# A two-layer attention kernel on one core: the second product of four units issued in one piece at the end of each step

## The chip, the cores and the metric

The kernel runs on one core of a Trainium2 chip. The metric is device time in microseconds (us) for one execution of the whole program; lower is better. The kernel before has a median of 1084.87 us over three runs (1084.28 to 1086.7).

## What is computed

Two transformer layers over one sequence of 2048 tokens with 128 channels, in float32, with an adaptive layer norm (scale and shift from a condition vector) ahead of every block.

- Layer 0 attention: 16 heads of width 8, over all 2048 keys, no mask. For each head `softmax(q k^T / sqrt(8)) v`, then an output product.
- Layer 0 feed-forward: a router picks one of 16 experts for each token; the chosen expert (`up * silu(gate)`, then down) and a shared expert of width 512 are added.
- Layer 1 attention: 8 query heads of width 16 with one shared key and value head, causal.
- Layer 1 feed-forward: a token-shifted channel mix with a squared ReLU and a sigmoid gate.

Only the attention of layer 0 is touched by the change. Its core is, for 512 queries and four heads at a time:

```python
w = jnp.einsum('bshd,bzhd->bhsz', q, k) / jnp.sqrt(jnp.float32(DV))
w = jax.nn.softmax(w, axis=-1)
vw = jnp.einsum('bhsz,bzhd->bshd', w, v)      # the second product
```

## The kernel before

**Units and steps.** Layer 0's attention is cut into 16 units (numbers 0 to 15). A unit is 512 queries and four heads. A unit has 16 steps, one for each block of 128 keys. The steps of layer 0 are numbered 0 to 255 in the program's order, so units 12 to 15 are steps 192 to 255. Layer 1 follows with eight units.

**What a step does for each unit.** A step J forms the scores of its 128 keys against 512 queries, turned so that keys lie on the partitions. That is done in two pairs of heads, called `st` 0 and `st` 1 here (`emit_st`, L425; the matmuls are at L919). Each pair is two bf16 matmuls of 512 columns. They work in different rows of the array, and each fills one bank of PSUM. ScalarE (ACT) takes the exponential of each bank (L1464), one instruction a bank, four a step, into an SBUF tile `PT`, and so frees the bank.

The second product (`pv`, L931 to L948) multiplies the exponentials with the values and adds into the bank `O`. It is float32, one product for each of the four heads, placed in four column strips of the array. The profile counts two MATMUL instructions for each float32 product. The second product of step J is issued in step J+1 (`LAG = 1`).

**The row maxima.** The exponentials need the maximum of every row. For this the same scores are formed once more, untransposed, for a later unit: a "score tile" S (L878 for layer 0, L885 and L888 for layer 1). It is 128 queries by 512 keys for two heads, in a double bank S0 or S1. VectorE (DVE) reduces it (L1218) and so frees the bank. In steady state a step holds two S tiles for the unit after this one. Near the end of layer 0 there are none for seven steps (236 to 242), since layer 1's keys are not there yet. From step 243 the S tiles are layer 1's first ones, which are small.

**Banks.** The transposed scores and all small pieces of other work take the banks T0, T1 and T2 in turn (`next_t`, L84). A bank may be written again only when its reader has freed it. A pair `st` takes two of the three. So where nothing else takes a bank in between, one of the two banks of `st` 1 is the first bank of `st` 0 of the same step.

**The order of the work** is written out by a planner, `make_plan`. Every engine walks the one list `order` and does its own part of each entry, strictly in that order. Loop L499 writes the order for the steps. In layer 0, where a score tile is due (`k` over 0, from `rate`, L459), a step is:

`light work; [piece]; st 0; S; pv of J-1, queries 0-255; light work; [piece]; st 1; S; pv of J-1, queries 256-511`

Here a `[piece]` is at most one piece of other work that is due (`do_later`, L445). I call the slot ahead of `st` 1 the middle slot. The slot ahead of `st` 0 is the end slot of the step before, since it stands behind that step's last second product. Where no score tile is due (steps 236 to 242), and in layer 1, the second product is already issued in one piece at the end of the step (L530): `st 0; (S); [piece]; st 1; (S); pv of J-1, all 512 queries`.

**Pieces of other work in units 12 to 15:** turning and projecting the attention's output (L957, L967, L976), the layer norm's transpose (L834), the router's logits (L1009), sorting the tokens by expert (L1037 to L1042), the shared expert (`up`: L1017 and L1018, `down`: L1027), and the sorted experts: `m0` (a transpose, L1049, in a T bank, copied by ACT at L1548), `m1` (L1061, in an S bank) and `m2` (L1069, in a T bank, copied by ACT at L1558). Later come layer 1's projections (L847, L864). SyncE fetches the experts' weights and stores and loads sorted rows. GpSimd (POOL) scatters and gathers them.

Of the kernel before, what the change touches and what calls it, by code (L numbers as in the profile page):

```python
# [18 lines left out]
LAG = 1  # L19
# [23 lines left out]
def kts(L, u):  # L43
    return 16 if L == 0 else 4 * (UNITS[1][u][0] + 1)
# [66 lines left out]
def make_plan():  # L111
# [44 lines left out]
    def between(key, *a):  # L156

        b = next_s()
        P.take((key,) + a, b, (b + "a", b + "b"))
        if key in ("up", "m1"):  # L160
            P.gate[(key,) + a] = len(P.gate) + 1
        P.stage(key, *a)
# [190 lines left out]
    def may_score():  # L353
        if si[0] >= len(tiles):
            return False
        return may_begin(*tiles[si[0]][:2])

    def emit_s():
        if not may_score():
            return  # L360
        t = tiles[si[0]]
        si[0] += 1
        L, u = t[:2]
        between("s", *t)
        if si[0] == len(tiles) or tiles[si[0]][:2] != (L, u):
            P.stage("neg", L, u)

            def neg_turn():
                P.take(("neg", L, u), P.next_t())
                P.stage("neg_turn", L, u)  # L370
                out[L, u] = 1
            urgent.append((now[0] + 2, neg_turn))
# [16 lines left out]
    def finish(L, u):  # L389
        c, quad = UNITS[L][u]  # L390
        last = quad == QUADS[L] - 1
        if (L, u) == units[-1]:
            tail()
            return
        P.stage("os", L, u)

        def o_turn():
            (between if L == 1 and u < 6 else beside)("o_turn", L, u)
            if last:
                at(now[0] + (2 if u < 15 else 1), w_turn)  # L400

        def w_turn():
            beside("w_turn", L, c)
            at(now[0] + 1, y)

        def y():
            P.take(("y", L, c), P.next_t())
            P.stage("y", L, c, P.xb)
            after_chunk(L, c, now[0])
        at(now[0] + 2, o_turn)  # L410

    def emit_pv(J, halves):
        if not 0 <= J < len(steps):
            return
        L, u, kt = steps[J]
        if kt == 0 and halves[0] == 0:
            P.take(("o", L, u), "O", filled=False)
        P.stage("pv", L, J - STEPS0 * L, u, kt, halves)
        if halves[-1] == 1:
            P.pvs += 1  # L420
            if kt == kts(L, u) - 1:
                P.pv[L, u] = P.pvs
                finish(L, u)

    def emit_st(J, pair):  # L425
        if J >= len(steps):
            return
        L, u, kt = steps[J]
        j = J - STEPS0 * L
        if L == 1 and kt >= 4 * UNITS[1][u][0]:  # L430
            P.masks[L, j, pair] = len(P.masks) + 1
        if (L, u) == (1, 7):
            P.wide.add((L, j, pair))
            P.take(("st", L, j, 2 * pair), next_s())
        else:
            for i in range(2):
                P.take(("st", L, j, 2 * pair + i), P.next_t())
        P.stage("st", L, j, u, kt, pair)

    def do_light(half=0):  # L440
        for k in sorted(k for k in light if k <= now[0] + half):
            for fn in light.pop(k):
                fn()

    def do_later():  # L445

        if urgent and urgent[0][0] <= now[0]:
            urgent.pop(0)[1]()
            return
        for book in (later, after):  # L450
            k = min(book, default=now[0] + 1)
            if k <= now[0]:
                fn = book[k].pop(0)
                if not book[k]:
                    book.pop(k)
                fn()
                return

    def rate(L, J):  # L459

        k = 0
        for J2 in range(J, min(J + 24, len(steps))):
            due = sum(n for n, s0, of in zip(many, starts, units) if s0 - LEAD[of] <= J2 and may_begin(*of))
            k = max(k, -(-(due - si[0]) // (J2 - J + 1)))
        return min(k, MOST[L]) if may_score() else 0
# [33 lines left out]
    while J < len(steps) + LAG:  # L499
        L, u, _ = steps[min(J, len(steps) - 1)]  # L500
        do_light()
        if J == begun[L, u] and not out[L, u]:
            for _ in range(4):
                emit_s()
            do_later()
            now[0] += 1
            continue
        k = rate(L, J)
        do_later()
        emit_st(J, 0)  # L510
        if L == 0 and k:
            emit_s()
            emit_pv(J - LAG, (0,))
            do_light(0.5)
            do_later()
            emit_st(J, 1)
            for _ in range(k - 1):
                emit_s()
            emit_pv(J - LAG, (1,))
        else:  # L520
            if k:
                emit_s()
            do_light(0.5)
            do_later()
            emit_st(J, 1)
            if k > 1:
                emit_s()
            if (L, u) >= (0, 15):
                do_later()
            emit_pv(J - LAG, (0, 1))  # L530
            for _ in range(k - 2):
                emit_s()
        now[0] += 1
        J += 1
# [27 lines left out]
def adaln_two_layers(nc, A, out):  # L562
    ctx = ExitStack()
    P = make_plan()
    order, turn = P.order, P.turn
    with ctx:
# [1393 lines left out]
```

## Time and profile before

| | |
|---|---|
| median of the runs | 1084.87 us |
| the profiled execution | 1091.35 us |
| its span, first to last instruction | 1089.5 us |
| PE (TensorE matmul) busy | 1007.8 us, 93% |
| DVE busy | 896.7 us, 82% |
| ACT busy | 823.0 us, 76% |
| chain that ended last | PE 70%, DVE 11%, ACT 8% |
| the second product's matmuls in that chain (L948) | 26% |

The profiled execution is 6.5 us (0.6%) over the median of the runs and 1.85 us over its own span. Busy time is time in which an engine had an instruction in flight. Matmuls overlap one another at their ends, so the distance between two starts is the cost in a dense stretch, not the duration. In a row of the timeline the first number is the start in us from the beginning of the span, the second the time from the group's start to its end. What stands in square brackets is how long the engine had been idle, and what it waited for.

### The profile page before, as it was taken

The page shows a single profiled execution, that of the slowest core. Times are in us where ns is not written, and L with a number is a line of the kernel's source. Part 1 is how long each engine was busy: PE and PEld are TensorE (multiplying, and loading weights), DVE is VectorE, ACT ScalarE, POOL GpSimd, SP SyncE. Part 2 cuts the span into 40 slices and gives each one's busy share as a digit, 9 for nine tenths or more (in the row PEclk, how much of TensorE's full clock was granted, in tenths as well). Part 3 has the DMA queues.
Part 4 walks back from the last instruction along what each step waited for, and adds up shares of the span by engine and source line. Part 5 has one row for each costly group of instructions (what it writes and reads, how often), then busy time and mean ns, then how long its engine had stood idle before and what let it go on. Part 6 is the DMA issues. An engine that isn't in the chain of part 4 may idle for free.

```text
span 1089.5 us, 22136 instructions
## 1 busy us (share of the span) xinstructions
PE 1007.8 (93%) x8642; PEld 340.8 (31%) x8642; DVE 896.7 (82%) x1135; ACT 823.0 (76%) x1585; POOL 195.2 (18%) x370
## 2 busy tenths in 40 slices
PE   3979999999999999999998899989989998899997
PEld 2332222222222222222222244334343563323313
DVE  5899999999999999999988677775778767897503
ACT  3229999998999998999986587666755576656785
POOL 4533200003000003000023200231042113110102
PEclk9569999999999999999999899999999999999996
DMA  3470620100000000000001522105200431200000
GB/s 109 115 167 4 134 43 12 21 2 2 2 3 2 2 1 2 3 1 2 3 1 39 176 79 59 40 27 97 37 1 7 142 106 37 34 10 1 1 11 10
DMA packets 47693, 42.05 MB, mean 39 GB/s; under 512 B 6534, under 2 KB 45798, under 8 KB 47590
## 3 DMA queue, kind: packets, MB, share of 16 engines
q1 hardware_dynamic: 45190, 35.17, 13.1%
q0 software_dynamic: 1824, 5.25, 1.7%
q8 instruction: 69, 1.13, 0.4%
q14 instruction: 34, 0.28, 0.1%
q10 hardware_dynamic: 576, 0.23, 0.1%
HBM read 26.83 MB, written 13.30 MB: 37 GB/s over the span
## 4 chain that ended last, share of the span: by engine, by line
PE 70%; DVE 11%; ACT 8%; issue 4%; SPq 3%; DMA 2%; POOL 1%; another core or an unknown queue 1%; POOLq 0%; ACTq 0%; DVEq 0%
PE O L948 26%; PE T L919 14%; PE S L878 8%; DVE mx L1218 6%; ACT PT L1464 5%; PE S L885 4%; PE T L928 4%; PE S L1061 2%; SPq L1840 2%; PE S L1027 1%; ACT PT L1458 1%; PE S L1017 1%; PE T L1069 1%; PE S L928 1%; PE T L957 1%
## 5 line engine op out<-in xcount | busy, mean ns | idle before, releaser
L1218 DVE TENSOR_REDUCE mx<-S 128x2 f32<-128x1024 f32 (+2 forms) x672 | 759.6, 1180 | 79.5 <-PE S L878 31.5
L1464 ACT ACTIVATE PT<-T 128x512 f32<-128x512 f32 (+2 forms) x1280 | 675.8, 580 | 117.9 <-PE T L928 49.1
L948 PE MATMUL O<-PT,Va 128*9 128x256 f32 (+1 forms) x4032 | 317.7, 387 | 3.3 <-ACT Os L1499 3.3
L878 PE MATMUL S<-Ks,Qs 48*128 48x512 bf16 x1024 | 206.3, 396 | 17.4 <-DVE mx L1218 8.4
L919 PE MATMUL T<-Qs,Ks 51*128 51x512 bf16 x1024 | 202.1, 387 | 13.4 <-ACT PT L1464 8.1
L919 PEld LDWEIGHTS T<-Qs,Ks 51*128 51x128 bf16 x1024 | 56.1, 93 | 224.8 <-issue 128.8
L948 PEld LDWEIGHTS O<-PT,Va 128*9 128x9 f32 x4032 | 59.8, 88 | 207.1 <-issue 197.5
L885 PE MATMUL S<-K,Qs 96*128 96x512 bf16 (+3 forms) x320 | 89.4, 349 | 5.0 <-DVE mx L1218 3.9
L928 PE MATMUL T<-Qs,K 99*128 99x512 bf16 (+3 forms) x256 | 67.4, 344 | 12.0 <-ACT PT L1464 8.3
L948 PE MATMUL O<-PT,V 128*17 128x512 f32 (+3 forms) x640 | 74.9, 534 | 0.0
L878 PEld LDWEIGHTS S<-Ks,Qs 48*128 48x128 bf16 x1024 | 52.6, 95 | 41.1 <-DVE mx L1218 27.3
L1725 POOL CAST n<-nm 128x16 bf16<-128x16 f32 x24 | 5.5, 228 | 316.6 <-DVE nm L1226 316.4
L1631 POOL TENSOR_SCALAR_AFFINE_SELECT PT<-PT 128x256 f32<-128x256 f32 x64 | 25.8, 409 | 132.6 <-ACT PT L1464 103.8
L885 PEld LDWEIGHTS S<-K,Qs 96*128 96x128 bf16 x320 | 28.3, 97 | 48.2 <-DVE mx L1218 18.9
L1740 POOL TENSOR_TENSOR vw<-om,rl 128x128 f32<-128x128 f32 x16 | 6.5, 407 | 185.6 <-DVE rl L1232 185.6
L928 PEld LDWEIGHTS T<-Qs,K 99*128 99x128 bf16 x256 | 19.3, 98 | 49.7 <-issue 36.8
L1458 ACT ACTIVATE PT<-S 128x1024 f32<-128x1024 f32 (+3 forms) x32 | 28.4, 943 | 3.2 <-PE S L928 3.0
L888 PE MATMUL S<-mq,idb 128*128 128x128 bf16 x128 | 25.7, 220 | 0.0
L1181 DVE RECIPROCAL rl<-T 128x4 f32<-128x4 f32 x3 | 0.5, 170 | 28.7 <-PE T L984 28.7
L1785 POOL DMA_INDIRECT XP<-sorted_y,posu x16 | 15.8, 990 | 38.7 <-DMA sorted_y<-Vf 34.5
L1449 ACT ACTIVATE nrow<-T 12x512 bf16<-12x512 bf16 x24 | 14.1, 586 | 11.4 <-PE T L898 11.1
L1277 DVE SCALAR_TENSOR_TENSOR Vf<-Vf,S 128x512 f32<-128x512 f32 x16 | 10.9, 682 | 13.8 <-ACT Vf L1542 12.8
(283 smaller groups left out, 814.1 us busy)
## 6 DMA issues: line engine op xcount, KB each, us to landing
Qs<-in_L_ffn_experts SPq DMA_DIRECT2D x28, 192.0 KB, 2.7
Ks<-in_L_ffn_experts SPq DMA_DIRECT2D x20, 192.0 KB, 2.6
Vf<-sorted_x SPq DMA_DIRECT2D x12, 256.0 KB, 4.3
sorted_y<-Vf SPq DMA_DIRECT2D x12, 256.0 KB, 2.3
Qs<-rows_q SPq DMA_DIRECT2D x24, 128.0 KB, 4.5
rows_q<-q SPq DMA_DIRECT2D x7, 384.0 KB, 2.5
Qs<-rows_q SPq DMA_DIRECT2D x36, 64.0 KB
sorted_x<-XP POOLq DMA_DIRECT2D x1, 1792.0 KB, 10.7
```

Of the source, the lines that this page charges most:

```text
L878: m = e.matmul(two[:, i, :], Qs[r0:r0 + 48, hp, q0:q0 + 128], Ks[r0:r0 + 48, hp, CH * kb:CH * kb + CH], start=True, stop=True, tile_positi ...
L885: m = e.matmul(two[:, i, 0:n], Q1[0:96, 4 * quad + 2 * pair + i, q0:q0 + 128], K1[0:96, CH * kb:CH * kb + n], start=True, stop=True)
L888: m = e.matmul(two[:, i, n - 128:n], idb[:, :], mq[:, :], start=False, stop=True, skip_group_check=True)
L919: m = e.matmul(bank, Ks[r0:r0 + 51, hp, keys], Qs[r0:r0 + 51, hp, CH * c:CH * c + CH], start=True, stop=True, tile_position=(r0, 0))
L928: m = e.matmul(bank[:, lo:CH], K1[0:99, keys], Q1[0:99, 4 * quad + 2 * pair + i, CH * c + lo:CH * c + CH], start=True, stop=True)
L948: m = e.matmul(Ob[32 * g:32 * g + d1, lo:hi], v, PT[(2 * j + g // 2) % 4][:, p0 + lo:p0 + hi], start=(kt == 0 and halves[0] == 0), stop=Tr ...
L1061: m = e.matmul(two[:, h, 128 * k:128 * k + 128], w_of(g, 2 * p + k)[:, 128 * h:128 * h + 128], hS[p % 2][:, 128 * k:128 * k + 128], start= ...
L1218: e.tensor_reduce(mx[:, u % 2, h0:h0 + 2, kb], two[:, :, 0:n], AX.X, ALU.max).then_inc(free, 1)
L1458: e.activation(both, Sb[turn["st", L, j, 2 * pair][0]][:, :, lo:CH], ACT.Exp).then_inc(free, 1)
L1464: e.activation(PT[(2 * j + pair) % 4][:, CH * i + lo:CH * i + CH], bank[:, lo:CH], ACT.Exp).then_inc(free, 1)
L1631: e.affine_select(out=both, in_=both, compare_op=ALU.is_ge, fill=0.0, base=0, pattern=[[0, 2], [1, 128]], channel_multiplier=-1).then_inc( ...
L1840: e.dma_start(Ks[r0:r0 + 8 * many, heads, cols], src[:, heads, :]).then_inc(loaded, 16)
```

## The change

In steps of units 12 to 15 in which a score tile is due, the second product is no longer issued as two pieces (queries 0-255 between the first S tile and the middle slot, queries 256-511 at the end of the step). It is issued as one piece of 512 queries at the end of the step. Everything else keeps its place in the order, and the banks are taken in the same turn. Units 0 to 11 keep the two pieces.

```diff
         do_later()
         emit_st(J, 0)
         if L == 0 and k:
+
+            halves = ((0,), (1,)) if u < 12 else ((), (0, 1))
             emit_s()
-            emit_pv(J - LAG, (0,))
+            if halves[0]:
+                emit_pv(J - LAG, halves[0])
             do_light(0.5)
             do_later()
             emit_st(J, 1)
             for _ in range(k - 1):
                 emit_s()
-            emit_pv(J - LAG, (1,))
+            emit_pv(J - LAG, halves[1])
```

## Rows read from the trace of the kernel before

**Rows 1.** Busy time by window (us, each engine's busy us and instructions, PEclk): unit 11, unit 12.
```profile
504.50:542.10 37.60, 37.04 (x394) 8.58 (x392) 37.10 (x35) 35.87 (x68) 1.27 (x5) 1.00 0.01 2
542.10:590.80 48.70, 45.34 (x450) 14.22 (x446) 44.65 (x63) 39.54 (x76) 12.23 (x18) 1.00 0.01 3
```

**Rows 2.** The page's costliest group: operation, shapes, count, busy us, mean ns, idle before.
```profile
L1218 DVE TENSOR_REDUCE mx<-S 128x2 f32<-128x1024 f32 (+2 forms) x672 | 759.6, 1180 | 79.5 <-PE S L878 31.5
```

**Rows 3.** Timeline (start, us, engine, line): a step without pieces, TensorE, up to the next.
```profile
556.13 0.39 PE L919 MATMUL T<-Qs,Ks 51*128 51x512 bf16 x2
556.35 0.40 PE L878 MATMUL S<-Ks,Qs 48*128 48x512 bf16 x2
556.67 0.62 PE L948 MATMUL O<-PT,Va 128*9 128x256 f32 x8
557.23 0.39 PE L919 MATMUL T<-Qs,Ks 51*128 51x512 bf16 x2
...
558.39 0.39 PE L919 MATMUL T<-Qs,Ks 51*128 51x512 bf16 x2
```

**Rows 4.** Timeline, TensorE: step 238, in which the second product is already one piece.
```profile
721.23 0.39 PE L919 MATMUL T<-Qs,Ks 51*128 51x512 bf16 x2
722.39 0.39 PE L919 MATMUL T<-Qs,Ks 51*128 51x512 bf16 x2 [0.78 <-ACT PT L1464]
722.71 1.05 PE L948 MATMUL O<-PT,Va 128*9 128x512 f32 x8
723.69 0.66 PE L834 MATMUL T<-idf,XP 128*128 128x128 f32 x4
```

**Rows 5.** Timeline: a step with m0 and m2 in the middle slot, m1 at its end.
```profile
646.58 0.39 PE L919 MATMUL T<-Qs,Ks 51*128 51x512 bf16 x2
...
647.00 1.08 ACT L1464 ACTIVATE PT<-T 128x512 f32<-128x512 f32 x2 [0.38 <-PE T L919]
...
648.14 0.38 ACT L1548 ACTIVATE Vf<-T 128x256 f32<-128x256 f32 x1
...
648.67 0.39 PE L919 MATMUL T<-Qs,Ks 51*128 51x512 bf16 x2
...
649.76 1.16 PE L1061 MATMUL S<-Vf,Qs 128*128 128x128 f32 x8
...
650.85 0.39 PE L919 MATMUL T<-Qs,Ks 51*128 51x512 bf16 x2
```

**Rows 6.** Timeline, TensorE: start of step 192, first piece, last piece and end of step 203.
```profile
539.68 0.39 PE L919 MATMUL T<-Qs,Ks 51*128 51x512 bf16 x2
...
544.46 0.66 PE L957 MATMUL T<-idf,Os 128*128 128x128 f32 x4
...
572.20 1.12 PE L1017 MATMUL S<-hT,sgT 128*128 128x512 f32 x2
...
574.12 0.39 PE L919 MATMUL T<-Qs,Ks 51*128 51x512 bf16 x2
```

**Rows 7.** Timeline, TensorE: start of step 209, and a wait in step 212.
```profile
590.73 0.39 PE L919 MATMUL T<-Qs,Ks 51*128 51x512 bf16 x2
...
605.40 0.39 PE L919 MATMUL T<-Qs,Ks 51*128 51x512 bf16 x2 [1.00 <-issue]
```

**Rows 8.** Busy time by window, columns as in rows 1: the stretch at the lower clock.
```profile
612.00:618.00 6.00, 5.43 (x36) 0.75 (x34) 4.87 (x5) 3.44 (x7) 0.00 (x0) 0.50 1.07 300
```

**Rows 9.** Timeline, TensorE: starts of a step with m1 in the middle, and the next.
```profile
634.20 0.39 PE L919 MATMUL T<-Qs,Ks 51*128 51x512 bf16 x2
...
638.47 0.39 PE L919 MATMUL T<-Qs,Ks 51*128 51x512 bf16 x2
```

**Rows 10.** Timeline, TensorE: starts of the two pairs of a step of unit 15.
```profile
771.24 0.39 PE L919 MATMUL T<-Qs,Ks 51*128 51x512 bf16 x2
...
772.66 0.39 PE L919 MATMUL T<-Qs,Ks 51*128 51x512 bf16 x2
...
774.19 0.39 PE L919 MATMUL T<-Qs,Ks 51*128 51x512 bf16 x2
```

## The prediction

> **What bounds the kernel now.** I read the page's busy shares and chain of waits first: PE is 93% busy and holds most of the chain that ended last. Shares say nothing of one stage, so I then took busy time by window, one unit each. In unit 11, which has no other work, DVE is busy 37.10 of 37.60 us, PE 37.04 and ACT 35.87 [rows 1]: three engines are nearly full, and a step of 2.35 us is two reductions of 1.18 us [rows 2]. From unit 12 on there is other work. The unit takes 48.7 us, DVE has 4 us free, PE 3.4 us, ACT 9 us [rows 1]. From step 216 to the end of layer 0 the timeline shows TensorE nearly dense, so what lengthens its queue lengthens the kernel.
>
> Next I read one step as distances between starts. In a plain step `st` 0 costs 0.22 us, the S tile 0.32, a half of the second product 0.56, and then `st` 1 begins, 1.10 us after `st` 0; the next step begins 2.26 us after the first [rows 3]. TensorE's own part of this is 2 x (0.22 + 0.31 + 0.55) = 2.16 us.
>
> **Which steps change.** Units 12 to 15 are 64 steps. Steps 236 to 242 have no score tile due and already issue one piece. So 57 steps change.
>
> **What one merged piece costs.** In step 238 the merged product starts at 722.71, and the next instruction at 723.69: 0.98 us [rows 4]. Two halves are 2 x 0.55 = 1.10 us [rows 3]. TensorE's own work falls by 0.12 us a step, or 57 x 0.12 = 6.8 us in all. That is the whole gain. The Trainium skill (TensorE: Matmul & The Clock Gate, "Back-to-back issue gap") puts the fixed part of an isolated matmul at about 2.5 ns, by which merging would save only some 0.02 us a step for its eight instructions fewer; the rows show six times that, and by the page's figure the sum below would be 5.7 us higher.
>
> **What the half in the middle was covering.** `st` 1 needs two of three T banks, and with an empty middle slot one of them is the first bank of `st` 0. ACT starts the exponential 0.42 us after `st` 0 (647.00 against 646.58), two take 1.08 us together and overlap a little, so one runs about 0.6 us [rows 5]; then TensorE has to hear of it. In step 238, which has an empty middle slot, this sum is seen directly: `st` 1 starts 1.16 us after `st` 0, and TensorE was idle 0.78 us waiting for the exponential [rows 4]. So the shortest first half is 1.16 us whatever TensorE does. Now the S tile and the half product fill 1.08 of these 1.16 us. After the change only `st` 0 and S (0.53 us) lie there, and the other 0.63 us is idle, unless a piece stands in the middle slot. The second half of the step becomes 0.22 + 0.31 + 0.98 = 1.51 us, against 1.08: +0.43 us, whatever follows.
>
> So a step changes by 0.43 us plus (new first half - old first half). A step without a middle piece goes from 2.16 us of TensorE's time to 1.16 + 1.51 = 2.67 us, or +0.51 us, less the waits for DVE that it has today and that the slower pace hides.
>
> **No cover from elsewhere.** Nothing else is moved: no DMA, no ACT, DVE or POOL instruction changes its place, and SP's queue is untouched. On PE's queue the half is moved past the middle slot, `st` 1 and one S tile. Those three start earlier where their banks allow. The completion that ACT waits for (the whole product of the step before) is still at the end of the step.
>
> **The sum, by stretches.**
>
> *Steps 192 to 203* (12 steps, empty middle slots). From 539.68 to 574.12 they take 34.44 us [rows 6]. Behind them stand six pieces (0.59, 0.59, 1.09, 0.56, 1.00 and `up` with 1.92 us, from start to next start; the first and the last in [rows 6]): 5.75 us. After: 12 x 2.67 + 5.75 = 37.8 us. In three steps ACT first copies a piece and `st` 1 comes 0.17 to 0.35 us later than 1.16; these stay, 0.7 us. 38.5 - 34.4 = **+4.0 us**. The waits of today (34.44 - 12 x 2.16 - 5.75 = 2.8 us) are what DVE held back; at 2.67 us a step DVE needs 2.36 us and is no longer the limit.
>
> *Steps 204 to 208* (sorting and two `up` pieces). Waits for DVE of 0.3 to 0.8 us stand behind every `up`. Two of these five steps should gain about nothing (the rank sum in a middle slot takes the half's place, and a DVE wait swallows the rest), the others +0.1 to +0.4: **+0.9 us**, bounds 0 and 5 x 0.43 = 2.2.
>
> *Steps 209 to 215* (590.73 on [rows 7]). Here no engine is busy: PE waits 1.0 us for "issue" at 605.40 [rows 7] while ACT and DVE idle too and the DMA queues carry the expert weights, and then TensorE runs at half clock in 612 to 618 [rows 8]. What ends last is not TensorE's queue, so most of 7 x 0.43 = 3.0 us is absorbed; below nothing is possible too, if the half-clock stretch goes. I take **+1.0 us**, bounds -2 and +3.
>
> *Steps 216 and 217*: empty middle, dense PE, 0.48 and 0.43: **+0.9 us**.
>
> *Steps 218 to 220 and 228 to 232* (8 steps, `m1` in the middle). 4.27 us today [rows 9]. `m1` costs 1.09 us [rows 5], so the first half is 0.53 + 1.09 = 1.62 us, over 1.16: covered. The second S tile wants the bank of the first, whose reduction ends about 0.64 + 1.22 = 1.86 us in, and is then started at about 1.97 instead of 1.84. Total 1.97 + 0.31 + 0.98 + 1.00 = 4.26: **0**, bounds -1 (8 x 0.12) and +1.
>
> *Steps 221 to 226* (6 steps, `m0` and `m2` in the middle). 4.27 us today, `st` 1 at 2.09 without a wait [rows 5]. After: both exponentials run until 1.50, then ACT copies `m0` in 0.38 us [rows 5], and `st` 1 wants `m0`'s bank: 1.88 + 0.14 = 2.02. The first half stays almost as long although TensorE has less to do. Then 0.53 + 0.98 + 1.09 (`m1`) = 2.60 against 2.18 [rows 5]: 4.62, +0.35 each, **+2.1 us**; step 227 has a turn in the middle and both banks of `st` 0 wanted again: **+0.45**.
>
> *Steps 233 to 235*: +0.42 for the first; the other two wait for DVE between `up` pieces anyway, +0.1: **+0.5 us**.
>
> *Steps 243 to 255* (unit 15, layer 1's small S tiles). No wait in most of them. The first half is 1.36 us in the mean of twelve (1.42 in the one shown, 771.24 to 772.66 [rows 10]), since the S tile is longer for TensorE; it can fall to 1.16. 12 x 0.20 = 2.4 us are gained there, and 13 x 0.43 = 5.6 us lost: **+3.2 us**.
>
> Sum: 4.0 + 0.9 + 1.0 + 0.9 + 0 + 2.1 + 0.45 + 0.5 + 3.2 = **+13.0 us**. Against its own time the profiled execution would go from 1091.35 to about 1104.4, its span from 1089.5 to 1102.5. That execution is 6.5 us over the median, and the changed stretch does not hold that difference in a visible place, so I add 13.0 to the median: **1097.9 us**. With every stretch at its lower bound the sum is about +6, at its upper about +19.
>
> **Rivals.**
>
> *TensorE's own arithmetic decides (faster).* If ACT gave the bank back within the 0.53 us that remain, each step would simply lose 0.12 us: -6.8 us, 1078 us. For it: PE's chain share and its dense stretches. Against it: in step 238 the wait is there, 0.78 us [rows 4]. It decides only where a middle piece of over 0.63 us stands that needs no copy ahead of `st` 1, and that is 8 steps of 57. Chance 0.05.
>
> *The slack of units 12 and 13 swallows the loss.* DVE and the DMA stall set the pace to step 215, so that only the dense stretches pay (0.9 + 2.1 + 0.45 + 0.5 + 3.2 = 7.2 us): 1092 us. If the dense stretches too run at their lower bounds, with the 8 steps' gain of 1 us and some gain from the half-clock stretch, about +2, 1087 us. For it: DVE was busy 44.65 of 48.7 us in unit 12 [rows 1]. Against it: 2.67 us is more than DVE's 2.36. Chance 0.15, one in five of it within 0.2%.
>
> *The clock falls.* TensorE would be idle 0.6 us in every plain step. It had been idle often ahead of 612, and then ran at a granted clock of 0.50, 1.2 GHz, in 612 to 618 [rows 8]; at half the clock TensorE's 2.16 us of a plain step could double. Between nothing and 2.2 us more a step I take 1.5, since part falls into waits. If half of the first 24 steps ran so, 12 x 1.5 = 18 us would be added to 13: 1116 us. Against it: step 238 idles 0.78 us ahead of `st` 1, and its `st` still takes 0.39 us as in the plain step at full clock [rows 3, 4]. The Trainium skill (TensorE: Matmul & The Clock Gate, "A second HAM failure mode: psum-queue depth-cycling") says that short idle times between groups of matmuls which cycle through PSUM banks can make the clock swing between its two levels; by it this rival would be the likely one, and step 238, where just this pattern keeps the full clock, speaks against it. Chance 0.06.
>
> *The change does nothing.* If the planner had issued whole products already in these steps, the time would stay. The rows show 256-column products in 57 of the 64. Chance under 0.01; with small absorbed effects of other kinds I leave 0.03 to "no difference".
>
> *One sign more:* the half-clock stretch vanishes (-3 us) together with the slack's absorbing. That lands at 1085 to 1090 and shares the 0.15 above.
>
> **How the numbers follow.** Forecast as summed 0.71; slack swallows 0.15; clock falls 0.06; faster 0.05; nothing 0.03. A run of this kernel can tell about 0.2% (2.2 us) from no change. Faster by more: 0.06 (0.05 and a little of the absorbed case). Within 0.2%: 0.03 + 0.03 = 0.06. Slower by more: 0.88. The range runs from 1089.5 (half-way between the slack case's 1092 and 1087) to 1104.5 (all upper bounds); the faster case and the fallen clock lie outside it.
>
> **What the profile after should show.** (1) L948 in units 12 to 15 as 128x512 groups of about 1.05 us, about 57 more. (2) In plain steps of unit 12, `st` 1 at 1.16 us after `st` 0 with an idle time of some 0.6 us <-ACT PT L1464, and a step of 2.67 us. (3) Steps with `m0` and `m2` in the middle at about 4.6 us, with `m1` in the middle still near 4.27. (4) Steps of unit 15 near 3.1 to 3.2 on the same work instead of 2.95 for the one shown. (5) Layer 1 unchanged, only later. The prediction is wrong if `st` 1 starts well below 1.16 us after `st` 0, if the second half of a step is below 1.5 us, or if TensorE's clock falls in unit 12.

## The result and the profile after

The changed kernel takes 1098.97 us in the median (1097.14 to 1102.02), against 1085.36 us (1084.28 to 1086.7) for the kernel before on the same chip, four runs each. The ratio is 1.0138, interval 1.0122 to 1.0155: 13.6 us slower, where 13.0 were forecast. The profiled execution took 1100.52 us, its span is 1098.7 us.

First the counts. The groups of the second product in layer 0, shapes kept apart (operation, shapes, count, then busy us and mean ns, idle before), show that the change did what it says. The first two lines are after, the third before. Eight instructions are one whole product, so there are 65 of them (520) instead of 8 (64): 57 more.

```profile
L951 PE MATMUL O<-PT,Va 128*9 128x256 f32 x3056 | 237.9, 383 | 3.0 <-ACT Os L1502 3.0
L951 PE MATMUL O<-PT,Va 128*9 128x512 f32 x520 | 68.0, 595 | 0.0
```

```profile
L948 PE MATMUL O<-PT,Va 128*9 128x512 f32 x64 | 8.4, 595 | 0.0
```

The plain step that answers to [rows 3] is the same step 198, on the timeline of TensorE (start, us, engine, line, idle before):

```profile
559.54 0.39 PE L922 MATMUL T<-Qs,Ks 51*128 51x512 bf16 x2
559.76 0.38 PE L881 MATMUL S<-Ks,Qs 48*128 48x512 bf16 x2
560.70 0.39 PE L922 MATMUL T<-Qs,Ks 51*128 51x512 bf16 x2 [0.56 <-ACT PT L1467]
560.91 0.40 PE L881 MATMUL S<-Ks,Qs 48*128 48x512 bf16 x2
561.24 1.05 PE L951 MATMUL O<-PT,Va 128*9 128x512 f32 x8
562.22 0.39 PE L922 MATMUL T<-Qs,Ks 51*128 51x512 bf16 x2
```

The first half of the step, from `st` 0 to `st` 1, is 1.16 us (1.10 in [rows 3]) although TensorE has only 0.53 us of work in it; it stands idle 0.56 us until the exponential is done. The second half, up to the next `st` 0, is 1.52 us (1.16 in [rows 3]). The step is 2.68 us, against 2.26.

What TensorE's matmuls waited for in 540 to 640 us (total us, times, longest), after and then before:

```profile
PE T L922 <- ACT PT L1467: 14.7, 25, 0.9
```

```profile
PE T L919 <- ACT PT L1464: 2.2, 5, 1.1
```

The wait for ACT to give back a T bank has gone from 2.2 to 14.7 us in this stretch. (A second trace of the kernel before, introduced below, has 1.0 us there; the longest of the five waits stood in a disturbed step.) ACT itself is not fuller: in the window of [rows 1] that it calls unit 12, which is steps 193 to 208, it is busy 39.59 us, before 39.54, but these 16 steps take 52.9 us instead of 48.7, at full clock.

```profile
543.40:596.30 52.90, 43.15 (x322) 12.00 (x322) 45.29 (x63) 39.59 (x75) 12.60 (x18) 1.00 0.01 3
```

A step with `m0` and `m2` in the middle slot, which answers to [rows 5]: the second pair starts 1.93 us after the first, the step takes 4.53 us.

```profile
651.25 0.39 PE L922 MATMUL T<-Qs,Ks 51*128 51x512 bf16 x2
651.78 0.44 PE L1052 MATMUL T<-idf,Vf 128*128 128x128 f32 x2
652.34 0.69 PE L1072 MATMUL T<-Qs,Vf 128*128 128x128 f32 x4
...
653.18 0.39 PE L922 MATMUL T<-Qs,Ks 51*128 51x512 bf16 x2
653.72 1.05 PE L951 MATMUL O<-PT,Va 128*9 128x512 f32 x8
654.69 1.16 PE L1064 MATMUL S<-Vf,Qs 128*128 128x128 f32 x8
655.78 0.39 PE L922 MATMUL T<-Qs,Ks 51*128 51x512 bf16 x2
```

### The profile page after: what moved, and what is told of

It reads as the page before. It is cut to its first block, busy times and chain, and to the rows that moved or that the text cites. A ratio compares the mean times of both kernels' runs of the same rounds, so it can differ in the third digit from the quotient of the medians.

```text
span 1098.7 us, 21253 instructions
## 1 busy us (share of the span) xinstructions
PE 1003.0 (91%) x8186; PEld 335.8 (31%) x8186; DVE 896.8 (82%) x1135; ACT 821.9 (75%) x1585; POOL 195.5 (18%) x370
## 4 chain that ended last, share of the span: by engine, by line
PE 69%; DVE 11%; ACT 9%; issue 4%; SPq 3%; DMA 2%; POOL 1%; POOLq 0%; ACTq 0%; DVEq 0%
PE O L951 26%; PE T L922 14%; PE S L881 8%; DVE mx L1221 6%; ACT PT L1467 6%; PE S L888 4%; PE T L931 4%; PE S L1064 2%; PE S L1030 2%; SPq L1843 1%; ACT PT L1461 1%; PE S L1020 1%; DMA Ks<-rows_k 1%; PE S L931 1%; PE T L1072 1%
## 5 line engine op out<-in xcount | busy, mean ns | idle before, releaser
L951 PE MATMUL O<-PT,Va 128*9 128x256 f32 (+1 forms) x3576 | 305.9, 414 | 3.0 <-ACT Os L1502 3.0
L951 PEld LDWEIGHTS O<-PT,Va 128*9 128x9 f32 x3576 | 53.0, 88 | 185.2 <-issue 176.7
L1412 ACT ACTIVATE hT<-T,mc 128x512 f32<-128x512 f32 x15 | 11.6, 775 | 13.1 <-PE T L837 12.8
```

Source lines behind the costliest of these rows:

```text
L951: m = e.matmul(Ob[32 * g:32 * g + d1, lo:hi], v, PT[(2 * j + g // 2) % 4][:, p0 + lo:p0 + hi], start=(kt == 0 and halves[0] == 0), stop=Tr ...
```

## The experiments

Step lengths below are distances between the starts of `st` 0. The expectations use the stretches of the prediction. All times of a table are from one trace each.

### The kernel before, a second trace

The two first traces differ by only 9.2 us in span (5.4 us in steps 192 to 255), the medians by 13.6. Most of the missing part sits in one place: steps 209 to 215 took 33.66 us before and 27.80 us after. So the kernel before was traced again, unchanged.

> The kernel before once more, for a second trace. In its first trace steps 209 to 215 took 33.66 us against 27.80 after the change, with stalls of all engines at 604 and 608 us and a half clock from 612 to 619 us; that trace is also 6 us above the median of the plain runs. Theory (these 6 us are an accident of that one execution): the second trace shows steps 209 to 215 in 24 to 29 us, a profiled time of 1085 to 1088 us, and a difference to the changed kernel of about 13 us step by step. Rival (the stretch is always so slow before the change, and the change gains 6 us there which it loses elsewhere): again about 33 us.

Its profiled time is 1085.81 us, and steps 209 to 215 take 25.95 us. Busy time by window, 604 to 612 us, in the first trace and in this one:

```profile
604.00:612.00 8.00, 5.04 (x38) 1.31 (x30) 3.67 (x4) 3.67 (x7) 3.94 (x5) 1.00 0.42 134
```

```profile
604.00:612.00 8.00, 8.00 (x74) 2.28 (x66) 7.07 (x9) 6.45 (x13) 2.87 (x3) 1.00 0.60 189
```

In the first, PE, DVE and ACT are all held up (busy 5.04, 3.67 and 3.67 of 8 us) while expert weights are being fetched, and the half clock of [rows 8] follows. They are held up in turn rather than together: over steps 209 to 215 there is only 0.33 us in which none of the three is busy. In the second trace there is neither the hold-up nor the half clock. [Rows 7, 8] showed a disturbance that one execution has and another has not.

### The changed kernel, a second trace

> The changed kernel once more, for a second trace. Theory: every step of units 12 to 15 has the length of the first trace to 0.05 us, except where all engines stall together or the granted clock is 0.50; such places (737 to 741 and 918 to 922 us in the first) lie elsewhere or are gone. Rival (the half clock is the change's doing): it comes again at the same place, near 737 us.

Its profiled time is 1107.76 us. It ran on another chip than the first traces, one on which the kernel before takes 1093.17 us. Steps 192 to 208, 216 to 232 and 243 to 255 have the lengths of the first trace to 0.02 us a stretch. Now steps 209 to 215 take 34.95 us, with a half clock from 612 to 622, and step 235 takes 9.51 us instead of 8.61:

```profile
612.00:622.00 10.00, 8.58 (x24) 1.72 (x24) 6.04 (x7) 4.19 (x9) 0.00 (x0) 0.50 0.72 207
```

So the disturbance meets both kernels. The half clock at 737 us came again at 745, in the same step (241, not touched by the change), and cost the same 1.6 us. That much speaks for the rival. But a kernel below whose layer 0 is that of the kernel before has it in step 241 as well, and in the second trace of the kernel before it lies two steps later. So it is not the change's doing. The other three traces from this chip also have 30.4 to 32.7 us in steps 209 to 215, while none of the seven traces on the two chips where the kernel before takes 1083.9 and 1084.5 us has more than 26.1. Step 235 goes with it: it takes 9.1 to 9.8 us in the five traces with slow steps 209 to 215 (the first of the kernel before among them), and 8.5 to 8.6 us in the eight others. The disturbance is in all four traces of the one chip, in none of the seven of the two others, and in one of the two first traces; why is open.

With the two traces that have it in neither place side by side, the second before and the first after, the loss can be read stretch by stretch (us):

| steps | before | after | difference | forecast |
|---|---|---|---|---|
| 192 to 203 | 34.44 | 38.83 | +4.39 | +4.0 |
| 204 to 208 | 16.64 | 16.78 | +0.14 | +0.9 |
| 209 to 215 | 25.95 | 27.80 | +1.85 | +1.0 |
| 216, 217 | 5.53 | 6.10 | +0.57 | +0.9 |
| 218 to 220 and 228 to 232 | 33.01 | 32.33 | -0.68 | 0 |
| 221 to 226 | 25.63 | 27.34 | +1.71 | +2.1 |
| 227 | 3.77 | 4.17 | +0.40 | +0.45 |
| 233 to 235 | 19.35 | 19.97 | +0.62 | +0.5 |
| 236 to 242 | 35.06 | 36.68 | +1.62 (half clock) | 0 |
| 243 to 255 | 42.75 (half clock; 41.37 without) | 45.14 | +2.39 (+3.77) | +3.2 |
| all | 242.13 | 255.14 | +13.0 | +13.0 |

The value without half clock is the value of the five other traces of these steps with an unchanged unit 15 and no half clock in it. With both stretches at half clock taken out the sum is +12.8.

### Units 12 and 13 alone, units 14 and 15 alone

```diff
-            halves = ((0,), (1,)) if u < 12 else ((), (0, 1))
+            halves = ((0,), (1,)) if u < 12 or u > 13 else ((), (0, 1))
```

and, in the other kernel,

```diff
-            halves = ((0,), (1,)) if u < 12 else ((), (0, 1))
+            halves = ((0,), (1,)) if u < 14 else ((), (0, 1))
```

> The merged product in units 12 and 13 only (steps 192 to 223), two pieces again in units 14 and 15. Theory (a step without cover in the middle slot has a first half of at least 1.16 us and a second half longer by 0.43 us): the terms of the prediction for steps 192 to 223 are 4.0 + 0.9 + 1.0 + 0.9 + 0 + 3 x 0.35 = +7.9 us, so about 1093 us, and with steps 209 to 215 at their upper bound of +3 instead of +1, 1095 us. Rival (the slack of units 12 and 13 swallows the loss, and the dense stretches behind pay all of it): at most +3 us, under 1088.5 us. In the trace, plain steps of unit 12 are 2.67 us long and steps of units 14 and 15 as before.

> The merged product in units 14 and 15 only (steps 224 to 255). Theory: 3 x 0.27 (steps with m0 and m2 in the middle, as the trace after the change has them) + 0.4 (227) - 0.2 (228 to 232) + 0.5 (233 to 235) + 3.4 (unit 15) = about +5 us, 1090 us. It and the kernel with units 12 and 13 alone should add up to the whole loss of 13.6 us. Rival (the slack of units 12 and 13 swallows the loss, so nearly all of the 13.6 us comes from the dense stretches): +10 us or more, 1095 us.

Units 12 and 13: ratio 1.0049 (1.0034 to 1.0065), or +5.4 us (3.7 to 7.1). Units 14 and 15: 1.0059 (1.0032 to 1.0087), or +6.4 us (3.5 to 9.5). The two parts are of about the same size; the rival wanted less than 3 and more than 10. Together they are 11.8 us, which the intervals don't tell from 13.6. My 7.9 for the first part lies above its interval. Both traces come from the chip with the disturbance: steps 209 to 215 take 30.89 and 32.67 us in them, which is more scatter than the difference in question. The other steps have the lengths that the whole change gives them (192 to 203 in 38.83 us in the first, 243 to 255 in 45.15 us in the second). With steps 209 to 215, step 235 and the stretches at half clock left out, the two are 5.5 and 5.3 us longer than the kernel before. So the two parts are equal within what can be told.

### Exponentials of a quarter of the columns

To test that the wait is the bank's return and nothing else that the merged product delays, ACT's exponential was shortened in both kernels, in units 12 to 15 only. Three quarters of these exponentials are left out, so only times are read from these two kernels. Each was traced once: 1088.05 us for the changed one, 1084.09 us for the one before.

```diff
-                        e.activation(PT[(2 * j + pair) % 4][:, CH * i + lo:CH * i + CH], bank[:, lo:CH], ACT.Exp).then_inc(free, 1)
+                        hi = lo + 128 if L == 0 and u >= 12 else CH
+                        e.activation(PT[(2 * j + pair) % 4][:, CH * i + lo:CH * i + hi], bank[:, lo:hi], ACT.Exp).then_inc(free, 1)
```

> The changed kernel with the same short exponentials in units 12 to 15 (three quarters of them left out there). Theory (the idle time ahead of the second pair is the bank's return: 0.42 us to ACT's start, the exponential, 0.14 us back): the first half of plain steps falls from 1.16 to 0.42 + 0.27 + 0.14 = 0.83 us, plain steps from 2.68 to about 2.35 us where DVE takes over as the limit, and steps 192 to 203 from 38.8 to 35 to 36 us; steps with m0 and m2 in the middle fall from 4.54 to about 4.15 us. Rival (the second pair waits for something else that the merged product delays, such as the S bank or PT): the first half stays at 1.16 us, and steps 192 to 203 at 38 us or more.

> The kernel before, with the exponential of units 12 to 15 of layer 0 taken over 128 of the 512 columns of each bank only (three quarters of these exponentials are left out), so that a bank comes back sooner. Theory: steps 192 to 203 stay at 34 to 34.5 us, since DVE and TensorE set their pace, and first halves of plain steps stay at 1.09 us. Rival (ACT's exponentials as such set the pace): they get shorter by 2 us or more.

In the changed kernel (timeline, PE, ACT) the first half falls to 0.85 us, as the sum 0.42 + 0.27 + 0.14 = 0.83 said. The order of the work and the length of the second half, 1.51 us, are as they were:

```profile
559.40 0.39 PE L922 MATMUL T<-Qs,Ks 51*128 51x512 bf16 x2
559.83 0.45 ACT L1468 ACTIVATE PT<-T 128x128 f32<-128x128 f32 x2 [1.09 <-PE T L922]
560.25 0.39 PE L922 MATMUL T<-Qs,Ks 51*128 51x512 bf16 x2 [0.24 <-ACT PT L1468]
560.79 1.05 PE L951 MATMUL O<-PT,Va 128*9 128x512 f32 x8
561.76 0.39 PE L922 MATMUL T<-Qs,Ks 51*128 51x512 bf16 x2
```

Steps 192 to 203 take 35.70 us (38.83 with full exponentials), inside the 35 to 36 expected. The wait is the bank's return. The steps with `m0` and `m2` in the middle fall only to 4.32 us, where I had expected 4.15. In them DVE ends the product that `m2` reads (L1344) 0.95 us after `st` 0, `m2` starts 0.15 us later, and the second pair follows it. There another wait seems to take over; no run tests it.

In the kernel before the same cut brings 34.44 to 33.25 us. I had expected 34 at least, the rival 32.4 at most; it lies between. The plain steps there became 2.18 us, about TensorE's own 2.16, and the idle times of 0.18 to 0.36 us behind ACT in steps 196, 197 and 202 are gone (these steps are 0.24 to 0.32 us shorter). So of the 2.8 us of waits that the prediction put down to DVE in this stretch, ACT and the bank's return held at least 1.2. The wait for DVE in step 200 stayed (1.95 us in the first half, 1.72 with full exponentials).

### The whole product in the middle of the step

```diff
-            halves = ((0,), (1,)) if u < 12 else ((), (0, 1))
+            halves = ((0,), (1,)) if u < 12 else ((0, 1), ())
```

> The same merged product in units 12 to 15, but issued in the middle, between the first S tile and the middle slot, where the first half stood. Theory (a bank comes back 1.16 us after its pair was started, and work has to lie in that time): plain steps of unit 12 are again 1.51 + 1.16 = 2.67 us, but a piece in the end slot now covers the wait of the second half, so the steps with such pieces are shorter than after the change by up to 0.6 us; steps with m0 and m2 in the middle and m1 at the end are 4.14 us (4.27 before, 4.54 after), steps with m1 in the middle 4.13. In all +1 to +3 us on before, 1086 to 1088.5 us. Rival (the merged product itself is what costs, wherever it stands, since ACT waits longer for the release of PT or PE for the exponentials of the step before): as after the change, 1097 us or more.

Ratio 1.0086 (1.0038 to 1.0134), +9.4 us, where I had expected 1 to 3. The mirror image is there in the plain steps: the first half is 1.52 us and the second 1.17, and now it is `st` 0 that waits. Step 194, up to step 195:

```profile
544.17 0.39 PE L923 MATMUL T<-Qs,Ks 51*128 51x512 bf16 x2 [0.46 <-ACT PT L1468]
544.39 0.40 PE L882 MATMUL S<-Ks,Qs 48*128 48x512 bf16 x2
544.71 1.05 PE L952 MATMUL O<-PT,Va 128*9 128x512 f32 x8
545.69 0.39 PE L923 MATMUL T<-Qs,Ks 51*128 51x512 bf16 x2
545.92 0.38 PE L882 MATMUL S<-Ks,Qs 48*128 48x512 bf16 x2
546.86 0.39 PE L923 MATMUL T<-Qs,Ks 51*128 51x512 bf16 x2 [0.56 <-ACT PT L1468]
```

Steps 192 to 203 take 36.29 us, 2.5 less than after the change, since six of them have a piece in the end slot. Against the kernel before, the trace has +1.9 us there, +1.1 in 204 to 208, +0.8 in 216 and 217, +2.6 in 218 to 220 and 228 to 232, +0.3 in 227 and +1.9 in 243 to 255, and 0.2 less in 221 to 226. (Steps 209 to 215 and 235 are longer too, as in every trace of this chip, and can't be put down to the change.) What failed most is my view of the steps with `m1` in the middle and `m0`, `m2` at the end. I had them at 4.13 us; they take 4.54. The second half of one, PE and ACT:

```profile
674.41 0.39 PE L923 MATMUL T<-Qs,Ks 51*128 51x512 bf16 x2
674.64 0.38 PE L882 MATMUL S<-Ks,Qs 48*128 48x512 bf16 x2
674.84 1.08 ACT L1468 ACTIVATE PT<-T 128x512 f32<-128x512 f32 x2 [0.38 <-PE T L923]
...
674.95 0.44 PE L1053 MATMUL T<-idf,Vf 128*128 128x128 f32 x2
675.51 0.68 PE L1073 MATMUL T<-Qs,Vf 128*128 128x128 f32 x4
675.80 0.39 ACT L1552 ACTIVATE Vf<-T 128x256 f32<-128x256 f32 x1
...
676.34 0.39 PE L923 MATMUL T<-Qs,Ks 51*128 51x512 bf16 x2
```

`m0` (L1053) and `m2` (L1073) take T banks too. `m2` takes the first of the pair at 674.41 and so starts only at 675.51. And the pair at 676.34 wants `m0`'s bank, which ACT copies (L1552, 675.80, 0.39 us) only behind both exponentials; it follows that copy by 0.15 us. The second half is 1.93 us where TensorE has 0.53 + 1.00 of work. It is the wait that the prediction had worked out for steps 221 to 226, whose first half after the change is 1.93 us as well, and that I didn't carry over to this place. A piece covers the wait only if it doesn't lengthen the same turn of banks. The rival (the product costs wherever it stands) is not borne out as a mechanism, but its number was the closer one.

### The whole product in the middle of 17 steps

```diff
+            halves = ((0, 1), ()) if 217 <= J <= 233 else ((0,), (1,))
```

> The kernel before, with the product in one piece only in steps 217 to 233, issued in the middle between the first S tile and the middle slot; in these steps a piece of other work stands in the end slot and covers the wait for the bank. Theory: each of these 17 steps loses 0.12 to 0.14 us (4.27 to 4.14), about -2.2 us in all, 1083.1 us, ratio 0.998. Rival (something else in these steps sets their length, as the return of the bank did at the end): no change or slower, 1085.3 us or more.

1086.84 us, ratio 1.0021 (1.0008 to 1.0034): slower. It rests on the same wrong view as the kernel before it. Its trace: -0.17 us in steps 221 to 226, which have `m1` at the end, but +0.95 in 218 to 220, +1.62 in 228 to 232, +0.34 in 227 and +0.39 in 216 and 217, and -0.20 in 233.

### The product placed by what covers the bank's return

```diff
+            first, second = ((), (0, 1)) if J in (218, 219, 220, 228, 229, 230, 231, 232) else ((0, 1), ()) if 221 <= J <= 226 else ((0,), (1,))
...
+            apart = J in (236, 238)
+            if apart:
+                emit_pv(J - LAG, (0,))
...
-            emit_pv(J - LAG, (0, 1))
+            emit_pv(J - LAG, (1,) if apart else (0, 1))
```

> The kernel before, with the second product placed in layer 0 by what covers the bank's return: in one piece at the end in steps 218 to 220 and 228 to 232 (m1 in the middle slot), in one piece in the middle in steps 221 to 226 (m1 in the end slot), and in two pieces in steps 236 and 238, where nothing stands in the middle slot and one piece was issued before. Theory, from the step lengths seen so far: -0.7 us (0.04 each, and 0.4 in step 220), -0.2 us, and 2 x -0.4 us: -1.7 us, ratio 0.9985. Rival (these small differences are taken back by waits behind them): ratio 1.000 or more. Its trace decides step by step; the ratio's interval may be too wide.

1081.59 us, against 1083.9 us for the kernel before on this chip (it is the measure for the two kernels below too), ratio 0.9987 (0.9973 to 1.0000): at the edge of what can be told from no change. The trace says step by step what the ratio can't: -0.48 us in 218 to 220, -0.19 in 221 to 226, -0.21 in 228 to 232 and -0.39 in 236 to 242, and +0.08 in 227, in all -1.2 us against the -1.7 expected. Step 238 gained 0.32 us and step 236 only 0.07, where I had 0.4 for each. At the end of step 236 stands a small transpose in a T bank (L904), behind which TensorE waits 0.51 us for ACT: the second half stays 1.65 us in either order, as it does in steps 216, 217 and 220 (below).

### Two pieces in layer 1

```diff
+            apart = L == 1 and u < 7 and 0 < J < len(steps) and steps[J - 1][:2] == (1, u) and steps[J - 1][2] < 4 * UNITS[1][u][0]
+            if apart:
+                emit_pv(J - LAG, (0,))
             do_light(0.5)
             do_later()
             emit_st(J, 1)
...
-            emit_pv(J - LAG, (0, 1))
+            emit_pv(J - LAG, (1,) if apart else (0, 1))
```

> The kernel before, with the second product of layer 1 in two pieces in the steps below the diagonal of its first seven units (40 steps at most), where it was one piece at the end. A plain step of layer 1 (st 0, S, st 1, S, product) takes 3.11 us before: 1.16 us to the second pair, in which TensorE works 0.96 us, and 1.95 us behind it. Theory: with a half of 0.55 us in the middle the first half is 1.50 us, the second 1.50, so 3.00 us, -0.11 each where the middle slot is empty, +0.1 where a piece covers it already: -1 to -3 us, ratio 0.997 to 0.999. The gain is small since TensorE's own work in the first half is 0.96 us of 1.16 here, against 0.53 in layer 0. Rival (the rule of layer 0, two pieces are faster by 0.35 us a step, holds whatever TensorE has to do): 40 x 0.35 = -10 us or more.

1083.99 us, ratio 0.9997 (0.9986 to 1.0008): no change. A plain step falls from 3.11 us to 3.05. Before (first the pair, then the second pair, then the next step):

```profile
1005.26 0.61 PE L928 MATMUL T<-Qs,K 99*128 99x512 bf16 x2
...
1006.43 0.59 PE L928 MATMUL T<-Qs,K 99*128 99x512 bf16 x2
...
1008.37 0.60 PE L928 MATMUL T<-Qs,K 99*128 99x512 bf16 x2
```

In two pieces:

```profile
997.02 0.60 PE L931 MATMUL T<-Qs,K 99*128 99x512 bf16 x2
...
998.54 0.60 PE L931 MATMUL T<-Qs,K 99*128 99x512 bf16 x2
...
1000.07 0.61 PE L931 MATMUL T<-Qs,K 99*128 99x512 bf16 x2
```

The floor is the same (1.17 us here), but TensorE has 0.96 us of other work under it. A plain step gains 0.06 us where I had 0.11, and of the 1 to 3 us in all that I had expected nothing can be told (the interval is -1.5 to +0.9 us). The rival (-10 us) is out.

### Both together

> Both of the former together. Theory: their sum, -3 to -5 us, ratio 0.996. Rival: no more than the better of the two.

1081.89 us, ratio 0.9987 (0.9976 to 0.9998): the gain of the order by cover alone, as the rival said, and not the 3 to 5 us of the theory. It is the one whose interval lies below 1, and only just. So the order by cover betters the kernel before by about 0.1%, and the one in layer 1 adds nothing that can be told.

## Why the prediction was right, by its own steps

The mechanism was right, and the direction and the largest terms come from it. That the sum came within 0.3 us of the clean traces (+13.0 against +12.8) is in part luck: four stretches were set 1.9 us too low together and five 2.2 us too high.

- **57 steps change.** Right: 57 more whole products.
- **The floor of 1.16 us, read in step 238.** Right, and the term that carries the sum. It stands in every plain step of units 12 and 13 and in nine of the thirteen steps of unit 15 (1.15 to 1.17), and it moves with the length of the exponential (0.85 us), which shows its cause.
- **The second half +0.43 us.** The length is right: 1.52 us in a plain step against the 1.51 worked out. "Whatever follows" is not. The increase is 0.42 to 0.43 us where the old second half was dense, 0.36 in plain steps, which had waited 0.08 us there, and only 0.24 in steps 216 and 217 and 0.15 in step 220. Behind the product of these stands a small transpose that takes a T bank, and the floor was paid there already. Step 220, up to step 221, in the second trace of the kernel before:

```profile
633.28 0.39 PE L919 MATMUL T<-Qs,Ks 51*128 51x512 bf16 x2
...
634.26 0.39 PE L898 MATMUL T<-idb,n 128*12 128x128 bf16 x4
...
634.94 0.39 PE L919 MATMUL T<-Qs,Ks 51*128 51x512 bf16 x2 [0.29 <-ACT PT L1464]
```

With short exponentials the old second half of steps 216 and 217 falls from 1.65 to 1.46 us and that of step 220 from 1.65 to 1.29, which shows the wait.
- **Steps 192 to 203, +4.0.** +4.39. DVE's waits of before were hidden as forecast (the first half of step 200 fell from 1.72 to 1.17 us), and the 0.7 us that I carried for ACT's copies in steps 196, 197 and 202 stayed in full. What the term lacked is a fourth such step: in 193 ACT copies the output bank first (0.60 us), and the first half only fell from 1.44 to 1.36 us, 0.2 over the floor. The rest is a plain step of 2.68 us instead of 2.67, twelve times. The reading of the old waits was wrong in part: of the 2.8 us laid to DVE, at least 1.2 were ACT's and the bank's return.
- **Steps 204 to 208, +0.9.** +0.14, mis-sized within its bounds. The waits in this stretch swallowed nearly all of it: steps 204, 206 and 208 kept their lengths to 0.01 us, and 205 and 207 became 0.08 longer each, where three steps were to have 0.1 to 0.4.
- **Steps 209 to 215, +1.0.** +1.85 between undisturbed traces. The value was not far off, the reasoning wrong: I took the hold-up and the half clock of that trace for a property of the kernel, and "no engine is busy" was a misreading (ACT and DVE work in part of that wait of 1.0 us). In an undisturbed execution TensorE is full in steps 210 to 214 (busy 13.75 of 13.77 us before), and these pay in full, +2.1 us; step 209, which waits for other things, became 0.4 us shorter, and step 215 0.2 us longer.
- **Steps 216 and 217, +0.9.** +0.57: their second halves grew by 0.24 us each, not by 0.43, as said above.
- **Steps with `m1` in the middle, 0.** -0.68. Seven of the eight gain 0.04 us. Step 220, whose second half had waited for the bank before (above), gains 0.40, which I had lumped with the rest.
- **Steps 221 to 226, +0.35 each.** +0.38 in the first and +0.27 in the others. The mechanism (the second pair waits for `m0`'s copy) was right; it starts at 1.93 us, where I had 2.02.
- **Steps 243 to 255, +3.2.** +3.77 against undisturbed traces. The first half fell to 1.16 in nine steps; in three others, where a piece or a maximum is copied first, it is 1.31 or 1.51, so that 1.8 us were gained there and not 2.4.
- **The rivals.** TensorE's own arithmetic is refuted by the waits. The slack of units 12 and 13 swallowed little: units 12 and 13 alone cost 5.4 us, and only steps 204 to 208 behave as this rival said. The clock did not fall in unit 12: 0.56 us of idle time in every plain step, and 1.00 in the window 543 to 596. The Trainium skill's rule that short idle times between groups of matmuls which cycle through PSUM banks can make the clock swing (TensorE: Matmul & The Clock Gate, "A second HAM failure mode: psum-queue depth-cycling") did not show here.
- **The 6.5 us between the profiled execution and the median.** The prediction saw no place for them. They had one: steps 209 to 215, which took 7.7 us less in the second trace, and step 235, which took 1.3 us less. Adding the sum to the median, not to that execution, was right all the same.
- **"About +6" and "about +19" for all bounds.** The bounds that are written down add up to +8.2 and +17.4 only; the rest of that width has no source in the text.

## What to carry to other kernels

With three banks in turn and two taken at a time, the time from one matmul to the bank's return (here 1.16 us for 512 columns) is a floor for each half of the step, and independent work on TensorE has to lie under it in both halves. Before merging two pieces into one, compare the saving (0.12 us here) with what the piece was covering: the floor less the work that stays (0.63 us). Where the work that stays nearly fills the floor, as in layer 1 (0.96 of 1.17 us), the order makes next to no difference. And a piece that takes a bank of the same turn is a poor cover: its own bank has to come back too, behind the exponentials (1.93 us where TensorE had 1.53 of work).

## What the runs showed of the hardware

- **The bank's return is a sum of three parts**: ACT starts 0.42 us after the pair of matmuls, one exponential of 512 columns takes about 0.6 us, TensorE goes on 0.14 us later. With 128 columns the whole was 0.85 us. Where TensorE has work until then, the second pair starts as early as 1.09 us after the first (1.10 in [rows 3]), so some 0.07 us of the 1.16 seem to be paid only when it stands idle.
- **TensorE, DVE and ACT can all be held up in the same few us** while large transfers run: TensorE was idle 3 of 8 us in one execution and not at all in another of the same kernel, with SP fetching expert weights in both, and for the longest of these waits the profile names no instruction of the program ("issue", "remote"). Steps 209 to 215 took 30.4 to 34.95 us in five traces and 25.85 to 27.8 in the eight others; in two of the five no stretch at half clock stands near. I have no run that settles the cause.
- **Stretches at a granted clock of 0.50** (1.2 GHz), 3 to 10 us long, stood in the middle of 12 of 13 traces, one to three in each. They can lie at different places for one and the same kernel, and come in both kernels. One of 3.4 us cost 1.4 to 1.6 us in steps 236 to 255. A difference of that size between two single traces is therefore no finding; a second trace of each kernel tells.
